# Digit marks of the message stage laid out in pairs of items, column numbers stored doubled

## The reference

```python
t1 = feat @ W1
msg = t1[src] + feat[src] * feat[dst] @ W2
scale = jnp.sqrt(out_deg[src]) * jnp.sqrt(out_deg[dst])
msg = msg / scale[:, None]
agg = jax.ops.segment_sum(msg, dst, num_segments=n)
```

## Time and profile before

| | |
|---|---|
| time, median of 3 runs | 3295.45 us (3284.95 to 3309.99) |
| the profiled execution | 3265.55 us, span 3263.7 us |
| PE busy | 2560.5 us, 78% |
| DVE busy | 2328.9 us, 71% |
| ACT busy | 1272.4 us, 39% |
| POOL busy | 1479.5 us, 45% |
| the message stage's main loop | 2269.05 to 2895.00 us of the span |

### The profile page before, as it was taken

The page is one execution under the profiler, slowest core; times in us unless marked ns, Lnnn a source line. Parts: engine busy times, 40 slices in busy tenths (PEclk is TensorE's granted clock), DMA queues, the critical chain, the costliest instruction groups (busy, mean ns, idle before and its releaser), DMA issues. The chain is left out here.

```text
span 3263.7 us, 62541 instructions
## 1 busy us (share of the span) xinstructions
PE 2560.5 (78%) x18415; PEld 1871.5 (57%) x18415; DVE 2328.9 (71%) x4050; ACT 1272.4 (39%) x2934; POOL 1479.5 (45%) x1363
## 2 busy tenths in 40 slices
PE   0894888888888888888656498957999999977048
PEld 0442555555555555555445355647999998975035
DVE  8543778777888888877656477677998998956601
ACT  0341545455555555555412011155544444543011
POOL 4685777676777777777352143052000000024251
PEclk9996999999999999999866799978999999988579
DMA  6226888888888888888412432110000000011140
GB/s 160 64 80 178 243 248 249 248 249 244 251 248 249 247 252 248 248 250 248 127 52 80 127 110 91 45 52 14 12 9 11 11 10 11 11 46 43 30 137 22
DMA packets 252156, 428.60 MB, mean 131 GB/s; under 512 B 58711, under 2 KB 162496, under 8 KB 251875
## 3 DMA queue, kind: packets, MB, share of 16 engines
q0 software_dynamic: 91920, 235.61, 25.4%
q1 hardware_dynamic: 128512, 159.36, 16.6%
q10 hardware_dynamic: 31568, 31.62, 3.1%
HBM read 508.04 MB, written 155.53 MB: 203 GB/s over the span
## 5 line engine op out<-in xcount | busy, mean ns | idle before, releaser
L1104 POOL DMA_INDIRECT edge_kv<-scratch_kv,edge_idx x784 | 898.5, 1146 | 387.2 <-issue 196.9
L1459 PE MATMUL edge_ps_o<-edge_vals,edge_onehot 128*128 128x264 f32 x1568 | 441.4, 404 | 49.0 <-ACT edge_rows L1318 37.2
L2914 PE MATMUL msg_ps_o<-all_fp,msg_at 125*123 125x256 bf16 x3375 | 437.4, 278 | 19.8 <-ACT msg_at L2967 16.3
L1129 DVE TENSOR_TENSOR edge_prod<-edge_ps_q,edge_kv 128x512 f32<-128x512 f32 x392 | 253.4, 685 | 273.4 <-PE edge_ps_q L1374 185.5
L1318 ACT ACTIVATE edge_rows<-edge_ps_o 128x264 f32<-128x264 f32 x784 | 287.5, 393 | 382.9 <-PE edge_ps_o L1459 319.5
L2914 PEld LDWEIGHTS msg_ps_o<-all_fp,msg_at 125*123 125x123 bf16 x3375 | 373.8, 138 | 26.1 <-ACT msg_at L2967 19.4
L1459 PEld LDWEIGHTS edge_ps_o<-edge_vals,edge_onehot 128*128 128x128 f32 x1568 | 263.1, 190 | 210.8 <-ACT edge_rows L1318 127.3
L1238 ACT ACTIVATE edge_hid<-edge_ps_h,edge_b 128x512 f32<-128x512 f32 x392 | 248.8, 684 | 188.0 <-remote 82.1
L2939 POOL TENSOR_TENSOR msg_x<-msg_x,msg_b 125x256 f32<-125x256 f32 x25 | 29.7, 1188 | 615.5 <-PE msg_ps_n L2890 615.5
L1374 PE MATMUL edge_ps_q<-edge_qw,edge_slots 128*128 128x256 bf16 x2352 | 298.8, 278 | 8.1 <-DMA edge_qw<-scratch_qc 6.7
L3026 DVE TENSOR_TENSOR msg_lom<-all_colb,msg_lo_t 128x1500 bf16<-128x1500 bf16 (+1 forms) x180 | 271.9, 1510 | 23.8 <-PE msg_ps_a L2866 5.1
(11 more groups left out here) (534 smaller groups left out, 4355.0 us busy)
## 6 DMA issues: line engine op xcount, KB each, us to landing
edge_qw<-scratch_qc SPq DMA_DIRECT2D x980, 192.0 KB
scratch_part<-edge_rows ACTq DMA_DIRECT2D x196, 396.0 KB
scratch_part<-edge_rows ACTq DMA_DIRECT2D x196, 132.0 KB
edge_ef<-in_edge_t_dram SPq DMA_DIRECT2D x98, 256.0 KB
edge_sgb<-scratch_seg SPq DMA_DIRECT2D x98, 256.0 KB
ffn_w<-in_L_ffn_w_dram SPq DMA_DIRECT2D x18, 1024.0 KB, 8.3
edge_kv<-scratch_kv,edge_idx POOLq DMA_INDIRECT x784
scratch_kv<-tab_kvrow SPq DMA_DIRECT2D x25, 250.0 KB
```

The source lines that it names most:

```text
L1104: pool.indirect_dma_start(kv[p][:, t, :], None, K.kv_d, bass.IndirectOffsetOnAxis(ap=idx[p][:, t:t + 1], axis=0)).then_inc(rows_in[p][q], 16)
L1129: dve.tensor_tensor(prod[:, 2 * h:2 * h + 2, :], ps_q[h][:].rearrange("e (t d) -> e t d", t=2), kv[pp][:, s * QT + 2 * h:s * QT + 2 * h + ...
L1459: pe.matmul(ps_o[t % 2][:, 0:RW], onehot[q % 2][:, t, :], vals[q % 2][:, t, :], start=True, stop=True).then_inc(out_done, 1)
L2914: m = pe.matmul(ps_o[gl % 3][0:GR, 0:D], at[gl % 3][:, h, :], K.fp[:, h, k, :], start=h == 0 and k == 0, stop=h == NT - 1 and k == 2)
```

## The change

The marks of two neighbouring items are laid side by side: lom and com get the shape (pair of items, column, 2), so that the innermost dimension runs over the two items of a pair. `twice` holds every column number two times in a row and is made once at the stage's start by one DVE copy with a semaphore of its own. The comparison reads `twice` once for each pair (step one), the two digits of the pair again and again (innermost step one, count two), and writes with step one. A batch of 5 items is padded to 6, whose sixth is never counted. In the count matmuls an item's weights and moving operand are now every second element of a pair, a step of 4 bytes in place of 2.

```diff
-        lom = [sb(f"lom{j}", [EW, n, RT], BF16) for j, (_, n) in enumerate(BATCHES)]
-        com = [sb(f"com{j}", [EW, n, IC], BF16) for j, (_, n) in enumerate(BATCHES)]
+        lom = [sb(f"lom{j}", [EW, -(-n // 2), RT, 2], BF16) for j, (_, n) in enumerate(BATCHES)]
+        com = [sb(f"com{j}", [EW, -(-n // 2), IC, 2], BF16) for j, (_, n) in enumerate(BATCHES)]
+        twice = sb("twice", [EW, RT, 2], BF16)
...
-                    m = pe.matmul(ps_a[(NB * gl + b) % 3][0:RT, i * IC:(i + 1) * IC], lom[j][:, k, :], com[j][:, k, :],
+                    m = pe.matmul(ps_a[(NB * gl + b) % 3][0:RT, i * IC:(i + 1) * IC], lom[j][:, k // 2, :, k % 2], com[j][:, k // 2, :, k % 2],
                                   start=True, stop=True)
...
             dve.memset(eps[:], EPS).then_inc(w_in, 1)
+            dve.tensor_copy(twice[:], K.colb[:, 0:RT].unsqueeze(2).to_broadcast([EW, RT, 2])).then_inc(twice_ready, 1)
+            dve.wait_ge(twice_ready, 1)
...
+                n2 = -(-n // 2)
                 for out, width, digit in ((lom[j], RT, lo_t), (com[j], IC, code_t)):
-                    dve.tensor_tensor(out[:], K.colb[:, 0:width].unsqueeze(1).to_broadcast([EW, n, width]),
-                                      digit[:, bass.ds(g * GI + i0, n)].unsqueeze(2).to_broadcast([EW, n, width]),
-                                      ALU.is_equal).then_inc(marked, 1)
+                    dve.tensor_tensor(out[:], twice[:, 0:width, :].unsqueeze(1).to_broadcast([EW, n2, width, 2]),
+                                      digit[:, bass.ds(g * GI + i0, 2 * n2)].rearrange("e (k j) -> e k j", j=2).unsqueeze(2)
+                                      .to_broadcast([EW, n2, width, 2]), ALU.is_equal).then_inc(marked, 1)
```

More of the change, by code:

```diff
@@ L2768, in edge_messages @@
         marked = sem("marked")
+        twice_ready = sem("twice_ready")
         counted = sem("counted")
```

## The result

The changed kernel takes 3254.92 us in the median of 4 runs (3229.87 to 3264.50), the kernel before 3300.04 in the median of its 4 (3284.95 to 3309.99): a ratio of 0.9867, 95% interval 0.9829 to 0.9905, 45 us less. On a second chip the same pair gave 3095.39 against 3131.88, ratio 0.9890 (0.9873 to 0.9906), 36 us less. The profiled execution took 3248.31 us. The forecast was 3255 us, 40 less. So the time came out as foretold, and that it did so to the tenth is luck: the interval of the ratio allows anything from 31 to 56 us less, and the loop that the change is about gave 33 in the profiled execution, where about 40 were foretold.

What follows compares the result with a forecast made beforehand. PE, the busiest engine in the message stage, was taken to lose time to a late DVE. Gains of 33 + 7.6 + 1.0 us, less 1.5, rounded to 40, took 3295.5 to 3255 us; range 3232 to 3305.

Steps and rivals of the forecast that it cites:

- What bounds the stage: Message stage's main loop: PE has most work, losing 37.0 us idle and 9.6 us of clock to a late DVE.
- all seventeen stalls: PE stalls of 1.4 us or more in the message loop, all read as DVE's program being behind PE's.
- Step (1): DVE's lom and com comparisons: 0.525 ns per element instead of 1.05, saving 198 us of DVE time over the stage.
- Step (2): PE in the message loop regains 33 us idle and 7.6 us of clock, plus 1.0 us at the start.
- most it can be: Upper limit of PE's gain: 37.0 idle, 9.6 clock and 1.0 at the start, about 48 us.
- ACT's waits under 120: Sign in the profile after: ACT's waits for qlow and the variances fall from 198 us to under 120.
- Step (3): Count matmuls' loads and moving operands at a 4-byte step: 0 to 1 ns per load, 1.5 us in the sum.
- Rival D: Strided weight loads of the counts take 54 ns more each: 56 us slower, 3350 us; chance 0.14.
- Step (4): Small parts: the column-number copy, about 0.4 us, falls in a DVE wait; at worst 0.4 us added once.
- A: DVE relieved and PE's stalls in the message stage mostly gone: 3255 us, chance 0.62.
- C: Comparison stays at 1.05 ns per element, DVE has 9 us more work: 3300 us, chance 0.10.
- B: DVE faster but half of PE's stalls stay, half of the 40 us gained: 3275 us, chance 0.14.

Runs made afterwards that it cites:

- e5_layout: Changed kernel's paired layout and PE reads, but DVE compares item by item, digit repeated; 3293.61 us (one run), kernel before 3267.06.
- e2_odd: e1_even's digit tables begun one element later, so every digit operand begins at an odd element; 3311.60 us (one run).
- e1_even: Changed kernel with digits copied into tables of 42 columns a group, so every comparison starts even; 3249.34 us against 3296.27 for the kernel before, ratio 0.9851.
- e3_tiny: Paired layout, only the first group's marks made in full, each later comparison handling two elements; 3245.10 us (one run).
- e6_mixfirst: Kernel before with the mix work put ahead of the marks in each slot of DVE's program; 3270.75 us against 3267.06, ratio 1.0020.
- e4_packed: Changed kernel, but PE reads a packed run of marks (2-byte step) in each matmul and load; 3249.42 us (one run).

## Why the prediction was right, and which step was mis-sized

**What bounds the stage** was right. PE's stalls were DVE's lateness passed on by ACT. Put in order of the marks' time on DVE within the loop, the loops fall in line: 482 us gave 656.9 (e5_layout), 448 gave 631.8 (e2_odd), 439 gave 625.5 (before), 350 gave 592.8 and 587.3 (after), 254 gave 577.7 twice (e1_even), 55 gave 580.1 (e3_tiny). PE's idle time, which the clock moves less, goes the same way: 54.6, 38.8, 37.0, 10.8 and 10.95, 3.5 twice, 3.5. Steep at the top, flat at the bottom, with little moved but DVE's work. e6_mixfirst speaks against the order of the program as the cause. One reading was not right: I took all seventeen stalls of the kernel before for DVE's lateness, but two of them are the two "issue" stalls (3.4 us together) that every kernel keeps. And DVE's gaps in the loop were not all under 0.6 us: ten were longer, the longest 5.4, together 15 of 55 us.

**Step (1), the marks, is the term that was mis-sized.** I took 0.525 ns per element for all operands and 198 us saved. The value holds where it applies: 941 ns for 1500 elements, 932 foretold. It applies only to operands that begin at an even element, which is every second group; 90 us were saved. With every start even the marks take 261.5 us in the whole of e1_even's stage (254 in its loop), where 250 were foretold: the mean of a large one is 971 ns and not 932. The range of the step (0.2 us a group more, 6.5 less) held it; what was missing was the question whether all 360 comparisons are the same instruction. That was in the code: a group of 41 items, addressed as g * GI. No row of before could have shown it, since no two-source bf16 operation there ran at the double pace. The Trainium skill, in "Vector Engine (DVE) Microarchitecture Reference", Performance modes, says that 4-byte alignment makes no difference to a two-source operation at two results a cycle; here, with a digit operand in rows of two elements that are read again and again, it made all the difference (941 against 1720 ns, e1_even against e2_odd), and the measurement decides.

**Step (2), what PE gets back,** came out short in the changed kernel for want of step (1). Foretold for the loop were 33 us of idle time and 7.6 of clock; it got back 26.2 and 6.6 (idle 10.8 us, not under 10; the loop 592.8, not 583 to 588; 587.3 in the other profile, where the clock did not fall). That half of the saving on DVE gave back 26 of the 33.5 us of idle that can be had is because the curve is steep where it starts. A whole relief is e1_even: idle down by 33.5 us, as foretold, and PE's busy time down by 14.4 (588.99 to 574.64), where I had 7.6. The sum of the two, 48, equals my "most it can be", but not by its terms: that one took 37.0 of idle and 9.6 of clock. So with the marks as I had sized them the loop would have gained 48 and not 39, and with the marks as they were it gained 33: the forecast lies between by two errors that met. What brought the whole program from 33 to 45 us on the first chip is outside the loop; 1 us of it is the stall at the stage's start, the rest was not traced and is within the noise. ACT's waits under 120: 108.2. The 65 us that stay even in e3_tiny are the chain's own.

**Step (3), the strided reads,** was right in choosing the near end of its bounds and a little low in size: 138 ns a load, as foretold, but 13 ns more for a burst of six, some 2 ns a load, where 0 to 1 were taken; about 4 us of PE's time for the 1.5 in the sum. Rival D is shown wrong by the loads of the changed kernel itself and by e4_packed.

**Step (4)** held: the copy of 0.41 us lies in a wait. PE's stall of 1.00 us for the third batch is gone.

**The rivals.** A is what happened. C was true of every odd group, and e2_odd is C in full: 632 us, 6 longer than before where 9 were allowed. B foretold a half relief and gave "pairs run at less than double pace" for it: a half relief of DVE there was, but from half the instructions at the old pace, and it cost only a third of the loop's gain (33 of 48 us came).

## What to carry to other kernels

Before a vector operation is rewritten to run at two elements a cycle, list where each operand begins for every value of the loop's counter: with an odd number of items a group, half of them begin within a word, and a padded column is all it takes. In the profile do not trust a median over several shapes: here it read 942 ns with 66 of 135 large instructions at 1700 or more, and the mean of the one shape, 1326, gave them away. If an engine is just about the bound, the first relief gives back most: 88 us less on DVE took 26 us of PE's idle time, the next 95 took 7, the last 193 none. And before a difference of a few us between two loops is explained by waits, compare idle time and busy time: the same kernel's two loops lay 5.5 us apart with the same waits.

## What was not expected of the hardware

- A two-source bf16 comparison over 1500 elements takes 941 ns if the operand in rows of two begins on a 4-byte word, 1720 if it begins 2 bytes later, and the other two operands don't change.
- Writing its output with a step of 4 bytes instead of 2 costs 8% at one element a cycle (1861 against 1720 ns), while PE's reads at that step cost 13 ns in a burst of six loads (398 to 411), which the duration of a single load (138 ns in both) does not show.
- The same PE stall of 1.75 us was followed by a stretch at 1.2 GHz in one execution of the changed kernel and by none in another.
- Chips differ by more than the change does: 3296, 3267 and 3132 us for the kernel before on three of them. In the two profiles from the last one the stage of the edges takes 1215.6 us, against 1324 to 1345 elsewhere, while PE's idle time in the loop studied here stays within 0.2 us (3.5, 3.5 and 3.6 for the same program on three chips). Comparisons of whole times across chips would have been worthless.
